# Order of TensorE's work inside one step of the attention of a graph network: scores first, turns last

## What is computed

```
q = (x @ Wq.T + bq)[dst]
k = (x @ Wk.T + bk)[src] + edge_attr @ We.T
v = (x @ Wv.T + bv)[src] + edge_attr @ We.T
alpha = (q * k).sum(-1) / sqrt(128)
ex = exp(alpha - segment_max(alpha, dst)[dst])
w = ex / segment_sum(ex, dst)[dst]
agg = segment_sum(v * w[:, None], dst)
```

## Time and profile before

| | us |
|---|---|
| time, median of 3 runs | 5450.69 (5449.11 to 5458.61) |
| the profiled execution's span | 5449.7 |
| attention loop in it, from the first turn of rows to the last sums | 1263.2 to about 3555 |
| PE busy in the span | 4724.4 |
| POOL busy in the span | 2090.5 |
| VectorE busy in the span | 3769.9 |
| ScalarE busy in the span | 2201.9 |

### The profile page before, as it was taken

One profiled execution on the slowest core, in us unless ns is written; L12 is line 12 of the kernel. 1 busy time (PEld: TensorE's weight loads), 2 busy tenths in 40 slices (PEclk: granted clock), 3 DMA queues, 4 the chain that ended last, 5 costly groups with the idle time before them and its releaser, 6 DMA issues.

```text
span 5449.7 us, 102910 instructions
## 1 busy us (share of the span) xinstructions
PE 4724.4 (87%) x38199; PEld 3405.6 (62%) x38199; DVE 3769.9 (69%) x6411; ACT 2201.9 (40%) x4109; POOL 2090.5 (38%) x2152
## 2 busy tenths in 40 slices
PE   1299999957888898898889888859999999699997
PEld 0276666735777777777777777725555554356665
DVE  4888888837777777777777777739999997710001
ACT  0166666654555555555555555541222220200000
POOL 4212211006777777777777777700000000001110
PEclk6599999978999999999999999979999999899998
DMA  8156665527888888888888888837888887456664
GB/s 220 64 183 204 215 204 192 178 90 201 216 216 220 217 215 218 220 214 218 217 216 215 212 220 213 212 126 252 296 295 293 299 299 304 180 180 203 208 204 129
DMA packets 1235894, 1154.95 MB, mean 212 GB/s; under 512 B 466847, under 2 KB 1148819, under 8 KB 1206019
## 3 DMA queue, kind: packets, MB, share of 16 engines
q1 hardware_dynamic: 779992, 802.55, 45.9%
q10 hardware_dynamic: 367917, 193.82, 12.6%
q0 software_dynamic: 87488, 151.98, 11.8%
HBM read 691.95 MB, written 468.81 MB: 213 GB/s over the span
## 4 chain that ended last, share of the span: by engine, by line
PE 45%; SPq 18%; POOL 15%; issue 8%; DVE 8%; DMA 3%; ACT 2%; DVEq 0%; POOLq 0%; ACTq 0%
PE psum L1409 44%; POOL G L838 7%; POOL H L838 7%; SPq L629 4%; DVE R L861 4%; SPq L626 3%; SPq L632 3%; SPq L510 2%; SPq L637 2%; DMA H<-local_dst_pairs 1%; ACT H L1727 1%; DVE H L861 1%; SPq L488 1%; SPq L618 1%; POOL R L789 1%
## 5 line engine op out<-in xcount | busy, mean ns | idle before, releaser
L1727 ACT ACTIVATE HT<-psum 98x512 f32<-98x512 f32 (+2 forms) x1527 | 980.0, 680 | 373.5 <-PE psum L1409 307.8
L1409 PE MATMUL psum<-R,HT 128*128 128x384 bf16 x6076 | 1084.9, 326 | 3.8 <-DVEq L1398 3.8
L1727 ACT ACTIVATE H<-psum 128x512 f32<-128x512 f32 (+1 forms) x765 | 455.9, 597 | 1465.5 <-PE psum L1631 774.2
L1409 PE MATMUL psum<-R 128*128 128x98 bf16 (+3 forms) x6858 | 980.4, 281 | 70.3 <-DVE R L861 27.8
L838 POOL DMA_INDIRECT G<-gather_table,cols_pc x908 | 871.1, 959 | 408.2 <-issue 274.2
L838 POOL DMA_INDIRECT H<-gather_table,cols_pc x896 | 858.0, 958 | 273.2 <-issue 270.5
L1409 PE MATMUL psum<-R,ACC 128*98 128x128 bf16 x10752 | 779.0, 221 | 0.0
L1409 PEld LDWEIGHTS psum<-R,HT 128*128 128x128 bf16 x6076 | 566.9, 97 | 327.9 <-DVEq L1398 4.0
L1409 PEld LDWEIGHTS psum<-R,ACC 128*98 128x98 bf16 x10752 | 740.5, 125 | 0.4 <-DVE ACC L861 0.3
L1409 PEld LDWEIGHTS psum<-R 128*128 128x128 bf16 (+1 forms) x6858 | 566.4, 111 | 225.7 <-issue 36.8
L861 DVE TENSOR_TENSOR R<-ACC,G 128x2048 bf16<-128x2048 bf16 x592 | 620.3, 1096 | 117.7 <-PE psum L1409 112.9
(11 more groups left out here) (242 smaller groups left out, 5876.0 us busy)
## 6 DMA issues: line engine op xcount, KB each, us to landing
weighted_blocks<-HT ACTq DMA_DIRECT2D x224, 784.0 KB
adjacency_blocks<-HT SPq DMA_DIRECT2D x74, 1568.0 KB, 5.7
ACC<-weighted_blocks SPq DMA_DIRECT2D x37, 3136.0 KB, 10.9
R<-weighted_blocks SPq DMA_DIRECT2D x37, 3136.0 KB, 10.8
HT<-adjacency_blocks SPq DMA_DIRECT2D x50, 1568.0 KB, 6.6
H<-local_dst_pairs SPq DMA_DIRECT2D x113, 512.0 KB
weighted_blocks<-H SPq DMA_DIRECT2D x72, 784.0 KB
R<-attr_parts SPq DMA_DIRECT2D x451, 99.0 KB
```

What stands on the lines that cost most here:

```text
L1409: return nc.tensor.matmul(o, lhs_t, rhs, start=start, stop=stop)
L1727: return nc.scalar.activation(o, a, f, **kw)
```

## The change

Only the order of TensorE's list within a step changes. Before: sums, turns of exponentials, a build, scores, turns of rows, a build. After: scores, sums, a build, turns of exponentials, turns of rows, a build. No instruction is added, removed or given another wait, and the lists of the other engines stay as they were.

```
             for k in range(STEPS):
+                if k - 1 in range(GN):
+                    t.wait_ge(s_gt, k)
+                    if k >= 2:
+                        t.wait_ge(s_min, k - 1)
+                    t.wait_ge(s_qw[(k - 1) % AR], 48 * ((k - 1) // AR + 1))
+                    o = psum[:, 3, :]
+                    mm(o, extras[(k - 1) % AR], GX[:, (k - 1) % AR, :], stop=False)
+                    last_ins = mm(o, queries[:, (k - 1) % AR, :], GT[:, (k - 1) % 2, :, :].rearrange("p j e -> p (j e)"), start=False)
+                    last_ins.then_inc(s_row, 1)
                 if k - 4 in range(GN):
                     ...
                     last_ins.then_inc(s_use, 1)
+                if 2 * k - 5 in range(PRE_N):
+                    build_weighted(2 * k - 5)
                 if k - 3 in range(GN):
                     ...
                     last_ins.then_inc(s_et, 1)
-                if 2 * k - 5 in range(PRE_N):
-                    build_weighted(2 * k - 5)
-                if k - 1 in range(GN):
-                    ...
-                    last_ins.then_inc(s_row, 1)
                 if k in range(GN):
                     ...
                     last_ins.then_inc(s_t, 1)
                 if 2 * k - 4 in range(PRE_N):
                     build_weighted(2 * k - 4)
```

## The result

The changed kernel takes 5962.15 us (median of four runs, 5961.07 to 5965.48) against 5449.9 us for the kernel before, a ratio of 1.0928 (95% interval 1.0904 to 1.0953). Predicted were 5980 us, in a range of 5930 to 6110.

What follows compares the result with a forecast made beforehand. GpSimd's gathers were taken to pace the loop at 5.07 us a step; a ring of 6.25 us over 447 steps adds 527 us, the loop's end makes it 531, giving 5980 us (5930 to 6110).

Steps and rivals of the forecast that it cites:

- What bounds the loop before: Attention loop: GpSimd's gathers pace it, 5.05 us for the four of a step, against steps of 5.07 us.
- The ring: Waits from turns of exponentials through five ScalarE pieces, scores, sums and a build to the next turns: 6.25 us a step.
- The terms: Parts of a new step: ScalarE 3.44 us, TensorE's scores, sums and build 2.78, restart 0.03.
- ScalarE's part with its two hand-overs: From the start of the turns of exponentials, through ScalarE's five pieces, to the waiting scores: 3.44 us.
- The sums: TensorE's sums in each new step, between scores and build: 1.01 us.
- a restart behind a pause: Extra time of TensorE's first group behind its wait in every step: 0 to 0.05 us, taken as 0.03.
- The end of the loop: Last steps without builds, where scores of the last group wait for ScalarE again: 3 to 4 us more.
- Rival A: TensorE runs ready sums and build in the pause: 4.52 us a step, time stays at 5450 us; chance 0.02.
- Rival B: TensorE's pause in every step lowers its clock: 6050 us with a twentieth of steps, 7395 with all; chance 0.07.
- Rival C: VectorE's waits for the mask's DMA enter the ring: 96.7 to 149.2 us more, 6075 to 6130 us; chance 0.07.

Runs made afterwards that it cites:

- e10: Kernel before, with SyncE issuing the masks' loads two steps earlier: 5437.6 us, ratio 0.9992.
- e6: Kernel before, with one more ScalarE piece (copy of a constant tile) in every step: 5442.8 us, ratio 1.0003.
- e1: Changed kernel, with ScalarE's copy to GT moved ahead of the two build copies: 5549.5 us, ratio 1.0201.
- e3: Kernel before, with only the scores moved to the head and the build left behind the turns of exponentials: 5639.6 us, ratio 1.0363.
- e8: Changed kernel, with the first build moved to the head of TensorE's list, ahead of the scores: 5649.3 us, ratio 1.0326.
- e13: Changed kernel, with one more ScalarE piece and four matmuls in TensorE's pause in every step: 6048.1 us, ratio 1.1054.
- e2: Changed kernel, with ScalarE's copy to GT directly behind its copy of the turned exponentials: 5526.1 us, ratio 1.0166.
- e5: Changed kernel, with one more ScalarE piece in every step, directly ahead of the copy to GT: 6235.7 us, ratio 1.1465.
- e14: Changed kernel, with four matmuls put into TensorE's pause in every step: 5958.5 us, ratio 1.0891.

## Why the prediction was right

**What bounds the loop before** was right as far as it went: GpSimd. It was held up for 5.1 us only, e10 removed VectorE's waits for masks and TensorE's for VectorE without any gain, and e6 hid added work. What I did not read is SyncE. The chain of work that ended last, on the page of the kernel before, gives its issues more than GpSimd:

```profile
PE 45%; SPq 18%; POOL 15%; issue 8%; DVE 8%; DMA 3%; ACT 2%; DVEq 0%; POOLq 0%; ACTq 0%
```

and it waited for other engines for 2.7 us in all between 1300 and 3500 us. Whether it would hold the loop near 5.07 us if the gathers were faster no run shows. For the change this makes no difference: its ring of 6.20 us is the longest, and SyncE waits 384.7 us in it.

**The ring** was right in its members. e1, e3 and e8 took members out (the two build copies, a build), and e13 put one in; each moved the step by that member's own time (0.98 us for 0.96, 0.70 for 0.69, 0.20 for 0.20). That the scores, the sums and the other ScalarE pieces are members rests on the timeline, and on e2's usual step of 4.52 us for an expected 4.54; none of them was taken out by itself.

**The terms.** Between these two turns of rows of the changed kernel are 447 steps in 2773.3 us, 6.20 us each; predicted 6.25:

```profile
1279.95 0.60 PE L1651 MATMUL psum<-ident,G 128*128 128x128 f32 x4
...
4053.28 0.60 PE L1651 MATMUL psum<-ident,G 128*128 128x128 f32 x4
```

ScalarE's part with its two hand-overs was 3.46 (predicted 3.44), the scores 1.09 (1.08), the build 0.69 (0.69), the sums 0.95. The sums were the one term off: I took 1.01 from a step in which a build preceded them, and 0.03 for a restart behind a pause. Behind the scores they cost 0.95, and the restart added nothing that shows (scores 1.09). The trace of the kernel before had the fitting row at the loop's end, where sums stand behind scores as in the new order and cost 3550.22 - 3549.27 = 0.95:

```profile
3549.27 1.11 PE L1409 MATMUL psum<-G,H 128*128 128x139 f32 x8
3550.22 0.60 PE L1631 MATMUL psum<-ident,R 128*128 128x128 f32 x4
```

447 x 0.05 us is 20 us, about the difference of 18 between 5980 and 5962.

**The end of the loop** was guessed at 3 to 4 us. From the last turns of rows to the last sums it was 4064.32 - 4053.28 = 11.0 us, before 3553.85 - 3546.36 = 7.5: 3.5 us.

**Rival A** (ready work passes the waiting scores) is out by e8, and by the ring shown above: the turned exponentials were copied at 2707.76, so that by the profile nothing held the sums back, and still they ran behind the scores at 2711.07. The Trainium skill ("TensorE: Matmul & The Clock Gate", section "Step-by-step: what each phase is for") says that matmuls keep their order. The trace of the changed kernel agrees, as just read.

**Rival B** (clock) came true in two steps of the changed kernel, about 3.6 us, and in 115 steps of e5. I had given it 0.07 and argued from one single pause of 1.93 us, which the group behind it survived. The same trace has another pause of 1.93 us, and there the sums took 2.05 us instead of 1.17:

```profile
2134.60 0.85 PE L1651 MATMUL psum<-ident,H 128*128 128x128 f32 x4 [1.93 <-DMA H<-gather_table,cols_pc]
...
2136.53 2.05 PE L1409 MATMUL psum<-G,H 128*128 128x139 f32 x8
```

The clock fell 25 times in the old loop, which is what its mean of 0.98 says. One row that suits the forecast was no argument against B. In the changed kernel all but three pauses stayed at 1.72 to 1.74 us and the clock fell behind none of these; that a pause of this length is harmless was not known when the forecast was made, and in this the forecast was lucky.

**Rival C** (masks) did not come true: the changed loop has no wait for masks at all. But where the ring is short, as in e2, it was the first wait to come.

## What to carry to other kernels

In a loop whose engines each work a fixed list, follow every copy that hands work back: a step lasts at least as long as the longest ring of turns, copies and consumers, and moving a consumer ahead of the group that starts the copying engine's list puts that whole list into the ring. Repair it on the engine that copies (e1, e2) as well as on the one that waits, and put independent work (builds) into the pause, not between the waiting group and the next start of the ring. When one ring has been cut, expect no more than the next limit gives: here the gathers, and masks and queries that a faster loop finds late. Look at every engine for this, also at the one that only issues DMAs.

## What was not expected of the hardware

A pause of TensorE in every step had a sharp price. In the changed kernel the clock fell behind none of 442 pauses of 1.72 to 1.74 us and behind two of three pauses of 1.89 us. With 0.20 us more in every pause (e5) it fell behind 115 of 446, the granted clock was 0.94 over 2600 us, and about every fourth step took some 8.07 instead of 6.39 us. Four matmuls without any use, put into the pause, brought it back to 1.00 and saved 188 us. They shortened the pause and gave TensorE more to do at once; which of the two did it was not separated. A 0.20 us piece on another engine thus cost 0.6 us a step.

Two kernels bound by the ring and measured in different groups had nearly the same time (the changed one 5962.2 us, e14 5958.5 us, most of the difference being the two slow steps), while the kernel before took 5449.9, 5440.8, 5440.3 and 5475.7 us in its four groups, 0.6% apart. Its gathers also took 959 ns each on average and those of the changed one 949 ns, whose DMA share was 0.68 instead of 0.82.
